# Three hidden tiles of an MLP in halves of 256 tokens, one activation table loaded earlier, and new places for a recurrent layer's stages

## What is computed

```python
# layer 0: instance norm, 1x1 convolutions, attention of x on ctx, residual
A = softmax(einsum('bct,bcs->bts', Wn @ inorm(x) + bn, Wm @ inorm(ctx) + bm))
x = Wo @ einsum('bcs,bts->bct', Wl @ ctx + bl, A) + bo + x
# layer 1: attention with 32 query heads and 8 key/value heads, layer norm
x = layernorm(attend(x @ Wq + bq, ctx @ Wk + bk, ctx @ Wv + bv, mask) @ Wo + bo + x) * gamma + beta
# layer 2: latents x attend to [ctx, x], then an MLP, 256 -> 1024 -> 256
y = attend(x @ q_w + q_b, concat([ctx, x]) @ kv_w + kv_b, mask) @ out_w + out_b + x
x = gelu(rmsnorm(y, post) @ w1 + b1) @ w2 + b2 + x
# layer 3: recurrent block, its state taken from ctx
xa = ln(x); sx = shifted(xa) - xa
xk, xw, xv, xr, xg = xa + sx * (maa_stack + tanh((xa + sx*maa_x) @ maa_w1) @ maa_w2)   # five mixes
w = exp(-exp(time_decay + tanh(xw @ td_w1) @ td_w2)); r, k, v = xr @ Wr.T, xk @ Wk.T, xv @ Wv.T
for t in range(64):                            # per head, state s of 8 x 8
    a = k_t[:, None] * v_t[None, :]; out_t = r_t @ (u * a + s); s = a + w_t[:, None] * s
x1 = x + groupnorm(out) * silu(xg @ Wg.T) @ Wo.T
xc = ln(x1); xk2, xr2 = mixes of xc and its shift
x = x1 + sigmoid(xr2 @ Wfr.T) * (square(relu(xk2 @ Wfk.T)) @ Wfv.T)
```

## Time and profile before

| | |
|---|---|
| median of three runs | 1889.08 us |
| the profiled execution | 1890.01 us, span 1888.0 us |
| PE busy | 1640.7 us, 87% |
| DVE busy | 1215.1 us, 64% |
| ACT busy | 894.8 us, 47% |
| POOL busy | 780.4 us, 41% |
| the chain that ended last | PE 66%, DVE 14%, ACT 8%, POOL 6%, issue 4% |

### The profile page before, as it was taken

The page is one execution under the profiler, slowest core; times in us unless marked ns, Lnnn a source line. Parts: engine busy times, 40 slices in busy tenths (PEclk is TensorE's granted clock), DMA queues, the critical chain, the costliest instruction groups (busy, mean ns, idle before and its releaser), DMA issues.

```text
span 1888.0 us, 34749 instructions
## 1 busy us (share of the span) xinstructions
PE 1640.7 (87%) x13615; PEld 1023.1 (54%) x13615; DVE 1215.1 (64%) x2153; ACT 894.8 (47%) x1855; POOL 780.4 (41%) x871
## 2 busy tenths in 40 slices
PE   5898998899997898888988989889998889889735
PEld 3675555565564655655555655646456465555303
DVE  4742478655886468855687457864588646983483
ACT  4454554545544445545454456444555544554202
POOL 5631249404573147702485034840457214770000
PEclk9998898999999999999988999999999999999857
DMA  6001014200331005100141101410042100510060
GB/s 186 1 2 36 1 21 55 42 23 1 44 43 35 19 1 69 25 28 19 18 55 22 44 4 24 62 36 19 1 53 36 33 19 1 69 25 1 13 91 11
DMA packets 73567, 60.78 MB, mean 32 GB/s; under 512 B 38960, under 2 KB 56512, under 8 KB 73408
## 3 DMA queue, kind: packets, MB, share of 16 engines
q1 hardware_dynamic: 55648, 47.99, 17.4%
q10 hardware_dynamic: 17216, 10.55, 2.0%
q0 software_dynamic: 544, 0.03, 0.0%
HBM read 20.28 MB, written 4.19 MB: 13 GB/s over the span
## 4 chain that ended last, share of the span: by engine, by line
PE 66%; DVE 14%; ACT 8%; POOL 6%; issue 4%; DMA 0%; DVEq 0%; SPq 0%; ACTq 0%; POOLq 0%
PE bank L638 26%; PE bank L777 8%; PE bank L1019 6%; DVE late L1316 6%; PE bank L957 5%; PE bank L654 4%; PE bank L982 3%; PE bank L717 2%; POOL soft_ring L1685 2%; PE bank L910 2%; POOL late L1640 2%; ACT soft_ring L1149 2%; PE bank L975 1%; PE bank L886 1%; DVE late L1328 1%
## 5 line engine op out<-in xcount | busy, mean ns | idle before, releaser
L1685 POOL TENSOR_TENSOR soft_ring<-soft_ring,seg_max 128x512 f32<-128x512 f32 x256 | 282.0, 1117 | 304.5 <-DVE seg_max L1482 303.8
L1164 ACT ACTIVATE soft_ring<-soft_ring 128x512 f32<-128x512 f32 x256 | 159.9, 625 | 177.6 <-POOL soft_ring L1685 177.6
L1316 DVE TENSOR_TENSOR_SCAN late<-late 128x520 f32<-128x520 f32 x128 | 220.7, 1724 | 12.6 <-POOL late L1642 9.4
L777 PE MATMUL bank<-early 32*128 32x128 f32 (+2 forms) x1024 | 152.5, 416 | 38.8 <-ACT soft_ring L1149 36.0
L957 PE MATMUL bank<-ident,soft_ring 128*128 128x128 f32 x1024 | 166.2, 292 | 22.6 <-ACT soft_ring L1164 19.8
L1640 POOL TENSOR_TENSOR late<-late 128x520 f32<-128x520 f32 x112 | 174.6, 1559 | 15.7 <-DVE late L1316 15.4
L957 PEld LDWEIGHTS bank<-ident,soft_ring 128*128 128x128 f32 x1024 | 116.3, 146 | 102.8 <-issue 53.4
L1482 DVE TENSOR_REDUCE seg_max<-soft_ring 128x8 f32<-128x512 f32 (+1 forms) x256 | 166.6, 675 | 0.2
L1693 POOL TENSOR_SCALAR soft_ring<-soft_ring,rden 128x256 f32<-128x256 f32 x64 | 65.5, 1023 | 215.4 <-DVE rden L1444 215.4
L1047 ACT ACTIVATE late<-bank 128x512 f32<-128x512 f32 (+2 forms) x104 | 60.5, 595 | 158.6 <-PE bank L638 158.4
L638 PE MATMUL bank<-early,w 128*128 128x512 f32 x256 | 120.6, 622 | 15.9 <-ACT early L1221 15.9
(11 more groups left out here) (257 smaller groups left out, 3310.1 us busy)
## 6 DMA issues: line engine op xcount, KB each, us to landing
late<-late SPq DMA_DIRECT2D x128, 260.0 KB, 4.5
c<-in_ctx ACTq DMA_DIRECT2D x8, 512.0 KB, 4.1
x<-in_x ACTq DMA_DIRECT2D x8, 512.0 KB, 4.9
out_x<-late SPq DMA_DIRECT2D x8, 512.0 KB, 2.9
mask<-in_mask_Bx1xSxS_ff ACTq DMA_DIRECT2D x16, 128.0 KB, 3.9
mask<-in_mask_BxS_ik SPq DMA_DIRECT2D x8, 256.0 KB, 3.3
w<-in_L_xattn_mlp_w SPq DMA_DIRECT2D x2, 1024.0 KB, 9.6
wkv<-in_L_xattn_kv_w SPq DMA_DIRECT2D x1, 512.0 KB, 3.8
```

Of the source, the lines that this page charges most:

```text
L777: ins = mm(t[:, width * n:width * n + width], lhsT, rhs, start=True, stop=True)
L1164: af(soft[:, u % SOFT, :], soft[:, u % SOFT, :], ACT.Exp).then_inc(sig("exp"), 1)
L1316: nc.vector.tensor_tensor_scan(sj[:, n % 2, :], wP[:, k, :, :].rearrange("p b t -> p (b t)"), aj[:, n % 2, :], 0.0, ALU.mult, ALU.add).the ...
L1685: tt(s, s, seg_max[:, u % SOFT, 0:segs].unsqueeze(2).broadcast_to([128, segs, 512 // segs]), ALU.subtract).then_inc(sig("sub"), 1)
```

## The change

Three things change. The hidden tiles u0, u1 and u2 are computed in two halves of 256 tokens: those of tokens 0 to 255 are issued ahead of the transposes of xnT 1, since they need xnT 0 alone, the others behind them, into the same banks. ACT loads Gelu's table before it drains xnT 1, and not when the first Gelu comes. And the tables have other step numbers for nearly all stages of layer 3.

```diff
@@ -457,40 +457,40 @@
         PLACES = {
...
-            "shift": (14, 16, 12, 2),
+            "shift": (11, 15, 11, 2),
...
-            "gate": (127, 122, 123, 119),
+            "gate": (130, 129, 125, 123),
...
@@ -910,6 +910,21 @@
                                 ins = mm(t[:, 256 * b:256 * b + 256], hT[:, k, 2 * p + b, :, :], kv[:, 1, k, :], start=k == 0, stop=k == KT - 1)
                         ins.then_inc(full, 1)
 
+                HELD = 3
+
+                def hidden(n, h):
+
+                    drained(pe, ("xnT", h))
+                    if h == 0:
+                        t, full = fill(pe, "turn", ("u", n))
+                    else:
+                        b, _ = spot(("u", n))
+                        t, full = banks[b], sig(f"bank{b}_full")
+                    for k in range(KT):
+                        ins = mm(t[:, 256 * h:256 * h + 256], w1[:, k, 128 * n:128 * n + 128], xnT[:, h, k, :], start=k == 0, stop=k == KT - 1)
+                    if h == 1:
+                        ins.then_inc(full, 1)
+
                 def between(i):
                     if i == U0 + 2:
                         keys1()
@@ -931,6 +946,11 @@
                         if i == A1 + 8 * h + 20:
                             values2(h)
                         if i == A2 + 8 * h + 17:
+                            if h == 1:
+                                if before is None:
+                                    pe.wait_ge(sig("mlp_in"), 16 * 2)
+                                for n in range(HELD):
+                                    hidden(n, 0)
                             pe.wait_ge(sig("xh2_ready"), past("xh2_ready") + 2 * h + 2)
                             turn_half("xnT", xh, h)
 
@@ -1004,10 +1024,11 @@
                         project(pair_of(i - 11))
 
                 if before is None:
-                    pe.wait_ge(sig("mlp_in"), 16 * 2)
                     pe.wait_ge(sig("mix_in"), 16 * (2 + NMIX + 1))
-                drained(pe, ("xnT", 1))
-                for n in range(HID // 128):
+                for n in range(HELD):
+                    hidden(n, 1)
+                    step()
+                for n in range(HELD, HID // 128):
                     product(("u", n), 512, [(w1[:, k, 128 * n:128 * n + 128], xnT[:, :, k, :]) for k in range(KT)])
                     step()
                 for q in range(2):
@@ -1216,6 +1237,8 @@
                                 link(af(xh[:, p, :], xr[:, p, :], ACT.Square, accum_out=stats[:, p, 0:1]))
                             rsqrt(rstd[:, r], stats[:, r, 0], eps6, 1.0 / E, "rstd2_ready")
                         if i == A2 + 8 * h + 17:
+                            if h == 1:
+                                tables(GELU)
                             t, free = take(act, ("xnT", h))
                             for k in range(KT):
                                 ins = af(xnT[:, h, k, :], t[:, 256 * k:256 * k + 256], ACT.Identity, scale=v("post", k))
```

More of the change, by code:

```diff
@@ L459, in build @@
             "moments": (0, 0, 0, 0),
-            "normalize": (3, 10, 1, 1),
-            "turn": (11, 11, 5, 1),
-            "shift": (14, 16, 12, 2),
[L463 to L478, removed]
-            "gate": (127, 122, 123, 119),
[L480 to L487, removed]
+            "normalize": (5, 10, 1, 1),
+            "turn": (8, 11, 6, 1),
+            "shift": (11, 15, 11, 2),
+            "maa": (15, 15, 12, 6),
+            "mix 0": (18, 29, 19, 14),
+            "mix 1": (22, 32, 21, 16),
+            "td": (29, 33, 29, 17),
+            "k": (35, 33, 29, 17),
+            "mix 2": (35, 33, 35, 18),
+            "decay": (37, 36, 36, 20),
+            "v": (42, 40, 40, 21),
+            "mix 3": (42, 40, 42, 31),
+            "mix 4": (43, 40, 43, 33),
+            "r": (47, 44, 43, 39),
+            "g": (49, 49, 47, 41),
+            "r u k": (53, 52, 50, 41),
+            "bonus": (54, 52, 54, 52),
+            "center": (125, 124, 122, 114),
+            "variance": (128, 128, 125, 122),
+            "gate": (130, 129, 125, 123),
+            "project": (131, 133, 125, 128),
+            "moments 2": (131, 133, 125, 128),
+            "normalize 2": (131, 133, 125, 132),
+            "turn 2": (134, 133, 126, 135),
+            "shift 2": (138, 138, 128, 136),
+            "ffn k": (138, 138, 130, 136),
+            "ffn r": (138, 138, 136, 136),
+            "ffn v": (139, 138, 141, 137),
         }
         SCAN_PLACES = (
[4 rows of a table removed]
[4 rows of a table added]
         )
```

## The result

The changed kernel took 1861.95 us (median of four runs, 1861.21 to 1863.12) against 1888.64 for the kernel before: a ratio of 0.9846, with a 95% interval from 0.982 to 0.9873. That is a gain of 27 to 29 us where 15 were forecast. The direction and most waits came as forecast; the size did not.

What follows compares the result with a forecast made beforehand. PE was taken to set the end, with only its idle 21.6 us a group and clock losses to win. Seven groups at 1.65 gave 11.5, tail -0.8, group 0 +2.3, clock +2.0: 15.0 off 1889.1, 1874 us, range 1861 to 1894.

Steps and rivals of the forecast that it cites:

- The clock behind the waits of u: Lower TensorE clock in u's passes, group 0 and two others, costs 6.1 us; a third, 2, was credited.
- Group 0: First group, no center ahead of its MLP: first halves fill the wait on xh2, gaining 2.3 us.
- Term D: Early layer 0: maa's wait of 1.10 goes, mix 0 waits 1.0 for Tanh; a loss of 0.2 a group.
- Terms C and E: POOL's products and picks change places by one to three instructions; costed at nothing, covered by layer 2's wait.
- Term B: Scans' end: POOL's half 0 additions leave their place ahead of product 13; 0.75 us a group gained.
- Term A: MLP stage: 3.20 us of PE waits go and 2.1 come; 1.1 us a group gained.
- The tail: After the last group: starts with DVE's statistics behind ffn v, gives back half a group's gain, 0.8 us.
- R1: Rival: ACT's table loads become the bound, ffn r waits 2.6, clock loses 1.7; 16 us slower, 1905; chance 0.16.
- R3: Rival: waits and clock gain together, A 1.6, B 1.0, C 0.4, D 0; 1862 us; chance 0.13.

Runs made afterwards that it cites:

- places_only: The new step tables on the kernel before the change, without half tiles and with Gelu's load where it was; ratio 0.9917.
- pool_only: Only POOL's sums of half 0 moved behind the last three products of the scans, on the kernel before the change; ratio 1.0062.
- early_back: The changed kernel with the early stages (normalize, turn, shift, maa, mix 0, mix 1) back at their old places; ratio 0.9831.
- extra_loads: The changed kernel with two more table loads ahead of Tanh in ffn r; ratio 0.9966 to the kernel before the change.

## Why the prediction was right and wrong

PE's two timelines, cut at the same products in every group, say where the 28.5 us came from (us; seven groups, six for the MLP stage from center to the next group). The forecast's third of the clock's 6.1 us is put to the stages in which it lay.

| stretch | forecast | before | changed | gained |
|---|---|---|---|---|
| group 0 | 3.2 | 177.6 | 174.0 | 3.6 |
| early layers, to the scans' first pick (D) | -1.4 | 720.7 | 724.2 | -3.4 |
| scans, to the wait for xnT 0's transposes (C, E) | 0 | 360.5 | 352.3 | 8.2 |
| scans' end, from that wait to center (B) | 5.3 | 122.1 | 115.7 | 6.5 |
| MLP stage (A) | 7.2 | 303.9 | 292.9 | 11.0 |
| from the last center to the end | 0.9 | 189.1 | 186.5 | 2.6 |

Two steps failed, and they hold most of the difference.

**Terms C and E** were put at nothing, between a loss of 0.8 and a gain of 0.4 a group, because what is late there was to be covered by the wait of layer 2's values (L910). That wait stood in two of the seven groups alone, 1.6 us in all, and is gone. The stretch of these places is 8.2 us shorter, 1.2 a group: 5.2 of idle time and 3.0 of busy time. PE's waits in it for layer 2's softmax (`soft_ring`) fell from 24.7 to 17.0 us. The four profiles with the old scan places took 355.7 to 366.4 us for it, the ten with the new ones 347.4 to 355.4. No run has these places alone, so which of them did it stays open.

**The clock behind the waits of u.** "The wait of 1.05 may or may not end this; I take a third, 2" failed too: it ended it in every group. After waits of 0.93 the second halves take 2.86 us in all seven groups, and the stage that took 52.4 before is as short as the others. In group 0 the passes of u take 14.4 us for 16.9. So nearly all of the 6.1 came.

**Term A** came out as worked, wait by wait: 0.93 for 1.05 at the second halves, 0.55 for 0.65 at project, nothing for xh4, 0.17 at ffn v for 0.4 in two places; 48.8 us from center to the next group where the working gave 49.0. The gain is 1.5 a group instead of 1.1. But its account rests on the halves, and places_only has the same stage without them: the number was right in part by luck. The working followed the changed kernel alone and never asked what project's start would be without the first halves; since that start hangs on ACT (drain, transfers, Gelu, load, Ln, Exp) and DVE's gate, 0.6 saved ahead of it came back as 0.55 at project.

**Term B** came near in its sum, 6.5 for 5.3, and not in its parts, so that is partly luck. Out 7's waits fell by 10.5 us in the seven groups, 1.5 each where 0.7 to 1.2 was forecast, and those of xnT 0's transposes, which it did not price, rose by 7.2. It also left out the clock behind the wait of out 7, though the earlier trace rows showed 0.53 there. From out 7 to center PE was busy 25.9 us before and is now 21.7. Only 0.9 of that came as time, since PE then waits for the scans' reads.

On the lock of the Trainium skill ("SBUF — State Buffer", "Who interferes with whom"): the rows agree with the page's "fully blocks". In pool_only the first normalization takes 1.12 us and the second 1.37, for 0.35 alone; each began beside a POOL instruction and ended 0.15 after it. A scan, too, that begins beside one POOL TENSOR_TENSOR ends 1.10 us after it (60 of 63 such scans in the trace of before, the others 1.09), and takes 1.22 to 1.24 alone. The prediction's "slowed from 0.72 to 1.2 each beside a scan, not stopped" was the mean of two: the first addition took 0.77, the second, held until the scan had ended, 1.65. The price of company showed most on the normalizations, where it was not looked for, and 0.3 on the last scan (1.53).

**Term D** has the sign forecast, but its -3.4 is no more than scatter: over the profiles with the new early places this stretch took 717.3 to 735.1 us, and early_back puts the term at nothing. The wait of mix 0 on which it rested did not come.

**Group 0** gained 3.6 us in these two profiles (177.6 to 174.0); over all profiles the means differ by 7.6. **The tail** gave nothing back: from the last group's start to the end 359.4 us became 356.7.

**R1** did not come, but by a hair: its price was right, and two loads more brought its wait. With the rest of the gain still there, that run is 0.3% below before and not 16 us above. The Trainium skill's drain of 1380 ns ("ScalarE: Activation LUTs", "What ACT_TABLE_LOAD costs") shows in no row: in the extra_loads run three loads in a row start at 1286.19, 1287.48 and 1288.77, and Tanh at 1290.06. **R3**, 1862, is the time that came, with A at 1.5 for its 1.6 and B at 0.9 for its 1.0; its C of 0.4 was too low as well.

What stays open, beside the scan places, is the scatter of the clock in the first 30 us of a group: in kernels whose program there is the same, nearly every group loses either 1.5 to 2.0 us or 3.7 (busy time by one less the granted clock, summed over windows of 2 us).

## What to carry to other kernels

Price a wait of the matrix engine by the granted clock of the stretch behind it, too: in extra_loads 2.6 us of wait cost another 1.4. But a higher clock saves time only where nothing else is late: from out 7 to center 4.3 us less of work gave 0.9. Before crediting an edit with a wait that goes, work out when the next thing that waits would start without it; if another engine's chain ends there, the wait only moves. An edit of the order on one engine (the POOL sums) was worth 10.0 us where it acts in one company and 4.2 in another, where the whole kernel got 0.6% slower, so it is to be tried in the company it will have, and its own stretch is to be read beside the total. A term put at nothing wants a reason that holds in every group.

## What the runs showed that was not expected

The same 13,711 passes kept PE busy between 1623.9 and 1647.7 us; nearly all of the difference is time at the lower clock. Two normalizations of 128 x 256 on DVE took 0.61 us when they began with POOL idle, 1.39 when the first began beside a POOL instruction and 2.41 when each did: each that began so ended 0.15 us after it. A table load followed another within 0.01 us.
